# A feed-forward layer's opening inside the mixing's tail, and outputs computed one pair later, on one Trainium2 core

## What is computed

```python
x = x + _L0_attn_ref(_layernorm(x), ...)
x = x + _L0_ffn_ref(_layernorm(x), ...)
x = x + _L1_attn_ref(_layernorm(x), ...)
x = x + _L1_ffn_ref(_layernorm(x), ...)

# first part of layer 0, inside: a recurrence over the tokens, 32 heads, state 32
bc = einsum('bti,oi->bto', value, W_bc)            # then each group of 32 is divided by its norm
z = S * (z - dt * A * s + dt * (Bz * u));  s = s + dt * z + dt * (Bx * u)
y = (Cz . z) + (Cx . s)
return einsum('bti,oi->bto', (y + skip * value) * silu(gate), W_out)

# second part
h = silu((x @ w1) * s1) * ((x @ w2) * s2)          # "up", 128 -> 512
h = gelu((h @ h1) * t1);  h = gelu((h @ h2) * t2)  # 512 -> 512, twice
return (h @ w3) * s3                               # "out", 512 -> 128
```

## Time and profile before

| | us |
|---|---|
| median of 3 runs | 1328.13 |
| lowest and highest of them | 1324.44, 1331.52 |
| the profiled execution | 1331.72 |
| its span, from the first instruction to the last | 1329.6 |
| PE busy in the span | 1279.4 (96%) |
| DVE busy | 910.6 (68%) |
| ACT busy | 651.5 (49%) |
| POOL busy | 588.8 (44%) |

### The profile page before, as it was taken

How to read it: one execution, slowest core, us unless ns; L and a number is a source line. 1 busy time by engine, 2 the same in 40 slices (tenths; PEclk the granted TensorE clock), 3 DMA queues, 4 the chain that set the end, 5 groups by cost and what they waited for, 6 DMA issues and landing times. The chain is left out here.

```text
span 1329.6 us, 23001 instructions
## 1 busy us (share of the span) xinstructions
PE 1279.4 (96%) x7802; PEld 705.5 (53%) x7802; DVE 910.6 (68%) x1771; ACT 651.5 (49%) x1564; POOL 588.8 (44%) x939
## 2 busy tenths in 40 slices
PE   7999998999999999998899998999999999999999
PEld 4443334566566566565445454555655556544545
DVE  6999996999999999997301206888787786630100
ACT  3265533566665665664322315665565666531221
POOL 2633323888888988987100002444444453500000
PEclk7989999999999999998899999999999999999999
DMA  3369897656656665664100002000000000000000
GB/s 99 127 264 394 338 393 273 215 191 224 201 201 212 220 203 196 223 213 167 64 0 0 1 0 90 1 1 1 1 1 1 2 1 1 1 0 0 16 0 16
DMA packets 72834, 151.38 MB, mean 114 GB/s; under 512 B 7312, under 2 KB 24336, under 8 KB 69904
## 3 DMA queue, kind: packets, MB, share of 16 engines
q1 hardware_dynamic: 66096, 133.66, 28.5%
q10 hardware_dynamic: 6624, 16.26, 3.2%
HBM read 98.78 MB, written 51.12 MB: 113 GB/s over the span
## 5 line engine op out<-in xcount | busy, mean ns | idle before, releaser
L1869 POOL TENSOR_SCALAR pr<-pr,rs,sg 128x512 f32<-128x512 f32 (+3 forms) x256 | 152.6, 614 | 204.9 <-DVE rs L1774 186.1
L720 PE MATMUL banks<-w_bc,valueT 128*128 128x512 f32 x392 | 185.1, 596 | 3.4 <-ACT ent L593 2.4
L1046 DVE TENSOR_TENSOR pp<-banks,ring 128x1024 f32<-128x1024 f32 x128 | 156.1, 1220 | 12.8 <-DVEq L1083 5.5
L1675 ACT ACTIVATE pr<-banks,nm 128x512 f32<-128x512 f32 (+3 forms) x256 | 132.8, 524 | 20.4 <-DVE nm L1768 17.7
L1663 ACT COPY prT<-banks 128x512 f32<-128x512 f32 (+3 forms) x128 | 54.3, 424 | 112.5 <-PE banks L1544 112.3
L1768 DVE TENSOR_REDUCE nm<-banks 128x2 f32<-128x1024 f32 (+3 forms) x128 | 105.5, 824 | 4.4
L1384 DVE TENSOR_TENSOR x<-x,banks 128x256 f32<-128x256 f32 x16 | 6.7, 421 | 148.3 <-PE banks L1295 148.3
L935 ACT COPY qk<-banks 128x512 f32<-128x512 f32 x128 | 74.8, 585 | 63.0 <-PE banks L834 63.0
L672 POOL TENSOR_TENSOR C<-abL,A 128x128 f32<-128x128 f32 x128 | 53.3, 424 | 104.9 <-DVE banks L347 91.8
L1544 PE MATMUL banks<-ident,pr 128*128 128x128 f32 x640 | 96.9, 281 | 2.1 <-POOL pr L1869 0.7
L1130 POOL TENSOR_SCALAR_AFFINE_SELECT bp<-bp 128x1024 f32<-128x1024 f32 x64 | 73.8, 1152 | 55.9 <-ACT bp L942 55.9
(11 more groups left out here) (254 smaller groups left out, 2499.6 us busy)
## 6 DMA issues: line engine op xcount, KB each, us to landing
ring<-psi SPq DMA_DIRECT2D x126, 512.0 KB, 4.4
psi<-ring SPq DMA_DIRECT2D x10, 2048.0 KB, 7.5
psi<-X SPq DMA_DIRECT2D x5, 2048.0 KB, 7.5
det<-w_bc ACTq DMA_DIRECT2D x16, 512.0 KB, 4.7
ring<-det SPq DMA_DIRECT2D x64, 128.0 KB, 4.7
bcs<-ent ACTq DMA_DIRECT2D x30, 256.0 KB, 6.9
ring<-bcs SPq DMA_DIRECT2D x30, 256.0 KB, 5.0
w_bc<-in_w_bc SPq DMA_DIRECT2D x4, 1024.0 KB, 10.9
```

The source lines that it names most:

```text
L720: mm = pe.matmul(bank, m["valueT"][:, c, t * P:(t + 1) * P], w, start=(c == 0), stop=(c == 1))
L1046: dve.tensor_tensor(pp[:, q % 2].rearrange("p (a c) n -> p a c n", c=2), sc.unsqueeze(2).broadcast_to([P, 4, 2, HN]), rec[:, n % RL, q % 2 ...
L1675: act.activation(pr[:, n % RP, h, 0:w], S[n % 2][:, h, 0:w], ACT.Exp, bias=nm[:, n % 4, h:h + 1], accum_out=sm[:, m % 3, n % 2, h:h + 1]). ...
L1869: pool.tensor_scalar(row, row, rs[:, n // 2 % 2, n % 2, h:h + 1], sg[:, TPB * b + it, hd:hd + 1], ALU.mult, ALU.mult).then_inc(s["scaled"], 1)
```

## The change

It has three parts.

**The layer's opening moves into the loop of `mix`**, for the first feed-forward layer only (`OPENED`). The turns of block 0 and 1 (`turn_first`), ScalarE's copies of them (`take_first`), the four up-products of block 0 (`up_first`), silus (`silu_first`) and gates (`gate_first`) are placed in the pairs 61 to 64 and after the loop, in banks 4 to 7. Their results lie in the memory of the ring of records (`opening_parts`), which now outlives `mix`; the second layer's attention uses the same memory for a buffer of its own. `ffn` sets its semaphores as if these steps had been done and begins with the turn of block 2. The first three weight transfers count on a semaphore of their own. ScalarE's square root for the last block moves behind the silus of block 1.

**TensorE's pair** becomes: scores of p, outputs of both units of p-1, first turn of p+1, projection, state and end of a half (even pairs, two pairs later than the half's last unit is put out), second turn, projection (even pairs). The state's transpose and the projection out go to free columns of bank YG. The loops run one pair longer. ScalarE takes YG in even pairs ahead of the copies of turns, spreads the state between the two copies of turns, and gets `expand_u` from GpSimd.

**GpSimd's pair** becomes combine, combine, gating, mask: the mask stands last, the gating (`evacuate`) comes from VectorE, and the factors C have three buffers (RC = 3) in place of two.

In the listings below, names in a row are of the memory that is written and read: `qk` is the scores' matmul, `bp,uz` and `qk,hz` the outputs, `ident,ct` and `ident,bp` a turn, `w_bc,valueT` a projection, `ident,hT` the state's transpose, `w_out,yg` the projection out.

TensorE before, in the middle of the loop: an odd pair, from its scores to the next pair's.

The diff, cut to its core:

```diff
@@ -727,13 +728,17 @@
     EARLY = TILES - TPB
     UNITS = TILES * HG
     PAIRS = UNITS // 2
-    RL, RB, RC, RQ = 3, 3, 2, 4
+    RL, RB, RC, RQ = 3, 3, 3, 4
...
@@ -821,12 +827,6 @@
                 pe.wait_ge(s["bt"], q + 1)
                 if q >= 1:
                     pe.wait_ge(s["qk"], q)
-                if q >= 10 and q % 4 == 2:
-                    t, f, j = split(q - 7)
-                    if passes_on(t):
-                        pe.wait_ge(s["hz"], 2 * (links(t, f) + 1))
-                    if f == 1:
-                        pe.wait_ge(s["oc"], t + 1)
...
                     if q > 0:
                         pe.wait_ge(s["ygc"], q // 4)
-                    if carried(t):
-                        pe.wait_ge(s["hz"], 2 * (links(t - 1, f) + 1))
+                    if q >= 8:
+                        ts, fs, js = split(q - 8)
+                        if passes_on(ts):
+                            pe.wait_ge(s["hz"], 2 * (links(ts, fs) + 1))
+                        if fs == 1:
+                            pe.wait_ge(s["oc"], ts + 1)
...
-                pe.transpose(TP[:, 0:P], hT[:, f].rearrange("p a n -> p (a n)"), k.ident[:]).then_inc(s["turned"], 1)
+                pe.transpose(YG[:, STATE:STATE + P], hT[:, f].rearrange("p a n -> p (a n)"), k.ident[:]).then_inc(s["turned"], 1)
...
+
+            def turn_first(b):
+                pe.wait_ge(s["prod"], UNITS - 2)
+                pe.wait_ge(s["row"], TPB * (b + 1))
+                for t in range(TPB):
+                    mm = pe.transpose(k.bank[4 + b][:, t * P:(t + 1) * P], rows[:, b * TPB + t], k.ident[:])
+                mm.then_inc(s["first_turned"], 1)
+
+            def up_first(c):
+                pe.wait_ge(s["first_xnT"], 2)
+                pe.wait_ge(k.ffn_first, FFN_FIRST)
+                pe.wait_ge(s["prod"], UNITS)
+                if c >= 2:
+                    pe.wait_ge(s["first_gated"], c - 1)
+                for n in range(2):
+                    mm = pe.matmul(k.bank[(6, 4)[c % 2] + n][:], first_w["w12"][:, n, c * P:(c + 1) * P], first_xnT[:, 0:T])
+                mm.then_inc(s["first_up"], 1)
...
-            for p in range(2 - LEAD, PAIRS + 2):
+            for p in range(2 - LEAD, PAIRS + 3):
                 if 0 <= p < PAIRS:
                     scores(2 * p)
                     scores(2 * p + 1)
+                if 1 <= p <= PAIRS:
+                    outputs(2 * p - 2)
+                    outputs(2 * p - 1)
+                if p == PAIRS - 1:
+                    up_first(1)
+                    up_first(2)
+                if p == PAIRS:
+                    up_first(3)
                 for u in range(2):
                     if 0 <= p + 1 < PAIRS:
                         turn_both(2 * p + 2 + u)
                     if 2 <= p + LEAD < PAIRS:
                         project(2 * (p + LEAD) + u)
-                if 0 <= p < PAIRS:
-                    outputs(2 * p)
-                if p >= 3 and p % 2 == 1:
-                    t, f, j = split(2 * (p - 2))
-                    pe.wait_ge(s["qk"], min(2 * p + 4, UNITS))
-                    if passes_on(t):
-                        turn_state(t, f)
-                    if f == 1:
-                        project_out(t)
-                if 0 <= p < PAIRS:
-                    outputs(2 * p + 1)
+                    if p == PAIRS - 3 and u == 0:
+                        turn_first(0)
+                        turn_first(1)
+                    if p == PAIRS - 2 and u == 0:
+                        up_first(0)
+                    if p >= 4 and p % 2 == 0 and u == 0:
+                        t, f, j = split(2 * (p - 4))
+                        pe.wait_ge(s["ygc"], min(p, PAIRS) // 2)
+                        if passes_on(t):
+                            turn_state(t, f)
+                        if f == 1:
+                            project_out(t)
...
+            def expand_u(t):
+                act.wait_ge(s["yg"], HG * (t - 1))
+                for f in range(2):
+                    dst = uz[:, t % 2, f].rearrange("p (j e) -> p j e", e=DIAG)[:, :, 0:P].rearrange(
+                        "p j (i e) -> p j i e", i=4)[:, :, :, 0:DH]
+                    act.copy(dst, m["u"][:, t, f * P:(f + 1) * P].rearrange("p (i j d) -> p j i d", i=4, j=4)
+                             ).then_inc(s["uz"], 1)
+
+            def take_first(b):
+                act.wait_ge(s["first_turned"], b + 1)
+                act.copy(first_xnT[:, b * T:(b + 1) * T], k.bank[4 + b][:]).then_inc(s["first_xnT"], 1)
+
+            def silu_first(c):
+                act.wait_ge(s["first_up"], c + 1)
+                if c >= 2:
+                    act.wait_ge(s["first_gated"], c - 1)
+                act.activation(first_g[:, c % 2], k.bank[(6, 4)[c % 2]][:], ACT.Silu,
+                               scale=first_w["s12"][:, 0, c:c + 1]).then_inc(s["first_silu"], 1)
...
-            for p in range(2 - LEAD, PAIRS + 2):
+            for p in range(2 - LEAD, PAIRS + 3):
                 if 0 <= p < PAIRS:
                     copy_scores(p)
                 if 2 <= p + LEAD - 1 < PAIRS:
                     root(p + LEAD - 1)
+                if 2 <= p <= PAIRS and p % 2 == 0:
+                    take(p // 2 - 1)
                 if 0 <= p + 1 < PAIRS:
                     copy_qk(2 * p + 2)
-                    copy_qk(2 * p + 3)
-                if 2 <= p + LEAD < PAIRS:
-                    square(p + LEAD)
-                if p >= 3 and p % 2 == 1:
-                    t, f, j = split(2 * (p - 2))
+                if p >= 4 and p % 2 == 0:
+                    t, f, j = split(2 * (p - 4))
                     if f == 1:
...
-                        act.copy(oc[:], TP[:, P:2 * P]).then_inc(s["oc"], 1)
-                if 0 <= p < PAIRS and p % 2 == 1:
-                    take(p // 2)
+                        act.copy(oc[:], YG[:, STATE + P:STATE + 2 * P]).then_inc(s["oc"], 1)
+                if 0 <= p + 1 < PAIRS:
+                    copy_qk(2 * p + 3)
+                if p == PAIRS - 3:
+                    take_first(0)
+                    take_first(1)
+                if p == PAIRS - 2:
+                    silu_first(0)
+                if p == PAIRS - 1:
+                    silu_first(1)
+                    silu_first(2)
+                if p == PAIRS:
+                    silu_first(3)
+                if 2 <= p + LEAD < PAIRS:
+                    square(p + LEAD)
+                if p >= 4 and p % 4 == 1 and p // 4 + 1 < TILES:
+                    expand_u(p // 4 + 1)
...
+            def gate_first(c):
+                dve.wait_ge(s["first_silu"], c + 1)
+                dve.scalar_tensor_tensor(out=first_ha[:, 0, c], in0=k.bank[(6, 4)[c % 2] + 1][:],
+                                         scalar=first_w["s12"][:, 1, c:c + 1], in1=first_g[:, c % 2], op0=ALU.mult,
+                                         op1=ALU.mult).then_inc(s["first_gated"], 1)
...
-                    evacuate(t, f)
                 if q % 2 == 0 and q // 2 % 16 == 12 and q // 2 >= 28:
                     invert(q // 32 - 1)
-            evacuate(TILES - 1, 0)
-            evacuate(TILES - 1, 1)
+            for c in range(HID // P):
+                gate_first(c)
...
+            def evacuate(t, f):
+                tok = slice(t * P, (t + 1) * P)
+                pool.wait_ge(s["ygc"], 2 * t + f + 1)
+                if t >= 2:
+                    pool.wait_ge(s["out"], t - 1)
+                pool.tensor_tensor(yg[:, t % 2, f], ygc[:, f, 2 * N:], m["gateT"][:, f, tok], ALU.mult).then_inc(s["yg_done"], 1)
...
             for p in range(-1, PAIRS):
                 if p + 1 < PAIRS:
                     combine(2 * p + 3)
+                if p + 2 < PAIRS:
+                    combine(2 * p + 4)
+                if p >= 3 and p % 2 == 1:
+                    t, f, j = split(2 * (p - 2))
+                    evacuate(t, f)
                 if p >= 0:
                     mask(p)
-                if p + 2 < PAIRS:
-                    combine(2 * p + 4)
                 if p >= 7 and p % 4 == 3:
                     residual(p // 4 - 1)
-                if p >= 4 and p % 4 == 1 and p // 4 + 1 < TILES:
-                    expand_u(p // 4 + 1)
                 if p >= 28 and p % 16 >= 12:
                     normalise(TPB * (p // 16 - 1) + p % 16 - 12)
+            evacuate(TILES - 1, 1)
             residual(TILES - 1)
 
...
-def load_ffn(sp, m, ins, loaded):
+def opening_parts(m):
+    flat = m["ring"][:]
+    slot = 2 * 8 * HN
+    return (flat[:, 0:2 * T].rearrange("p (r t) -> p r t", r=2),
+            flat[:, slot:3 * slot].rearrange("p (b c t) -> p b c t", b=2, c=HID // P))
...
+        sp.dma_start(w["w12"][:, j], ins[n]).then_inc(first, 16)
+    sp.dma_start(w["s12"], ins["s12"]).then_inc(first, 16)
...
+            if OPENED:
+                pe.sem_inc(s["turned"], 2)
+                pe.sem_inc(s["up"], KH)
+            else:
+                turn(0)
+                turn(1)
...
```

(9 more changed lines are left out.)

80 lines of the change are left out of this document (45 added, 35 removed).

## The result

The changed kernel takes **1353.35 us** (median of 6 runs, 1343.66 to 1359.38), the kernel before 1329.89 us in the same comparison (median of 6, 1324.44 to 1336.47): ratio 1.0183, 95% interval 1.0151 to 1.0215. It is 1.8% slower; the forecast was 1319.6 us, and the time lies outside the range of 1310 to 1333. The profiled execution of the changed kernel spans 1351.2 us, that of before 1329.6 us.

A forecast was written before the change was run, and what follows sets the result against it. The prediction took TensorE to bound the loop, 25.48 us a tile. From the profiled 1331.72 us, -9.8 + 2.8 - 1.5 gave 1323.2, and 3.6 less for the median 1319.6 us; range 1310 to 1333.

The forecast's parts named there:

- Part 3: Loop, outputs one pair later: TensorE's floor of 25.48 us a tile stays; 0 us, between -3 and +6.
- Part 5: Loop, gating moved from VectorE to GpSimd: VectorE loses 9.8 us but had time spare; 0 us.
- the cost that could undo this: Loop, shared way to memory: GpSimd operations hold VectorE's scaling L1023, making VectorE the bound; +19 us, chance 0.13.
- TensorE bounds the loop: Mid-loop tile: TensorE busy 25.48 of 25.48 us, VectorE second by 1.3 us a tile.
- Part 1: Opening of the first feed-forward layer: two turns and four up-products leave it; -9.8 us.
- Part 2: Mixing's tail: takes in the opening's 7.9 us of TensorE work, 5.1 covered; +2.8 us, ends +0.5 and +7.9.
- the hitch: Mixing's last 30 us: a VectorE operation took 4.80 us, usually 0.25; forecast to stay; rival that it goes, 1313.5 us, 0.17.
- Part 4: Loop, ScalarE's chain of copies: a draw with TensorE, 0 us; tiles with a batch's moments, -1.5 us.
- The rival's point of decision: Loop: mean time of L1023, 1.03 us, from which VectorE's holding would decide the time; chance of slower 0.13.
- The rival's time: Whole kernel if VectorE, held by GpSimd, needs 26.7 us a tile: +19 us, 1339 us; chance 0.13.

The follow-up runs named there:

- mask_waits: Changed kernel with one wait added: GpSimd's mask waits until VectorE has done the L1085 of that round; 1319.41 us, ratio 0.993.
- loop_only: Changed kernel with the layer's opening left where it was before, so only the loop is changed; 1354.50 us, ratio 1.0212.
- no_hitch: opening_only with four normalisations moved from pairs 60 to 63 to pairs 62 and 63, two each; 1316.63 us, ratio 0.9921.
- opening_only: Kernel before with only the layer's two turns and four up-products moved into the mixing's tail; 1321.76 us, ratio 0.9961.
- write_only: Changed kernel with GpSimd's mask replaced by a fill of zeros that reads nothing; 1316.90 us in one run.
- later_plain: Changed kernel with the mask between the two combines and the gating on VectorE, both as before; 1352.77 us, ratio 1.0175.
- two_buffers: Changed kernel with two buffers of factors instead of three; 1336.63 us, ratio 1.0061.

## Why the prediction was wrong, point by point

- **The step that failed** is the loop's term in the sum. Parts 3 and 5 put the later outputs, the mask at the end of GpSimd's round and the moved gating at 0 us each, and the cost that could undo this was argued away. The loop measured +33.6 us. In the changed kernel the mask starts 0.04 to 0.11 us ahead of L1085 and holds it for nearly all its length, VectorE's products are late, and TensorE idles 2.4 us in a carried tile; one wait that keeps the mask behind L1085 gives 34 us back (1353.35 to 1319.41).
- **TensorE bounds the loop** (first section): right for the kernel before, and right again with mask_waits, 25.40 of 25.46 us busy. In the changed kernel it no longer does.
- **Part 1, -9.8:** right, -9.3 (10.89 to 1.59 us).
- **Part 2, +2.8:** the tail grew by 1.7 us, but by luck: the hitch went at the same time. Against loop_only, where it is gone too, the opening's work costs 4.4 us (26.89 to 31.28); in the old loop, with the hitch in both, 0.45 (29.62 to 30.07). All lie within the stated ends, but for the last, just under +0.5. The working took 4.6 of the 10.5 us of TensorE's idle time as the hitch's, where the earlier trace rows give 3.15 in its window; without the hitch the tail of no_hitch is 4.3 us shorter than that of opening_only.
- **Part 3, later outputs, 0:** right as a statement on TensorE's parts: carried tiles of 25.45 us stand in mask_waits and write_only. Wrong as a price: with the mask and the gating where they were (later_plain), 31 us are lost against opening_only. It counted what the mask may wait for, "so the mask can stand last", and not what it meets; put last it costs 23 us.
- **Part 4, ScalarE's chain:** TensorE's wait for the even pair's copy did not come. The -1.5 for the tiles with moments did not come either. These are three sets of two tiles; before they took 51.8 us each, with mask_waits 51.6, 52.3 and 52.1 in order of time.
- **Part 5, the gating, 0:** mis-sized, in the other direction. On GpSimd instead of VectorE the gating gains 21 us with the mask last (1373.92 to 1353.35), 23 with it between the combines (1352.77 to 1330.18), 8 with the wait (1327.64 to 1319.41), and nothing in the loop of before (1316.63 and 1317.77). The third buffer, which was to pay for the mask standing last, costs 17 us there (1336.63 to 1353.35). The sign set down for part 5, TensorE waiting for VectorE's products in every tile, is what the trace shows: 18 times in 280 us, 22.1 us.
- **The cost that could undo this** named the right operation and the right mechanism and gave it 0.13. Its argument against, "L1023 comes after a root, and a block of 0.73 us is what most GpSimd operations can give", failed: it took the two engines as independent, so that a mask would be met by chance. They are coupled by waits, and with 2.06 and 2.26 us between common points they meet in the same phase in most rounds.
- **The rival's point of decision**, a mean of 1.03 us, was set too high. The loss was there at 0.947 us, since it left out the state's operations: L1117, L1121 and L1127 took up to 0.65 + 0.72 + 0.70 instead of 0.21 + 0.29 + 0.29 us, 1.28 us a set, with two sets a tile. It also took TensorE as waiting only when VectorE's sum passes its own; but TensorE waits in the even pair although VectorE has 1.2 us left in the tile (27.24 of 28.41).
- The rival's time, 1339 us, was 14 us short of 1353.35.
- **The hitch**: left where it is by the forecast. In fact it went in the tail, and two of the same kind came in the loop, 4.74 us each, at 445.39 and at 558.56.

## What to carry to other kernels

Where VectorE is within some per cent of the bound and GpSimd runs beside it, list VectorE's small SBUF operations with what GpSimd has running at their start, in the new order; a small operation costs what it meets, and not its own time. Look for the wait that couples the two engines and add up both ways from there: if the two ways end at the same moment, here within 0.04 us, what meets once meets in most rounds, and a single wait that orders the two can be worth more than the whole change. Such a wait is cheap only where the held-back result isn't wanted soon: here +44 us with outputs in the same pair and a combine behind the mask, -34 us with outputs one pair later and the mask last. And vary the parts in a square before calling them dependent: here two parts of 21 to 23 us nearly cancelled, and a third of 31 us stood behind them.

## What the runs showed of the hardware that was not expected

- A VectorE operation can be held over many GpSimd operations and not over one: 4.74 us over seven (445.39), 4.80 us in the kernel before and in opening_only. It is rare. In the changed kernel from pair 0 on, a VectorE operation that had waited over 0.02 us was let in at 118 of 130 ends of a GpSimd operation with another one right behind it; the 12 others all belong to the two holdings of 4.74 us. In the records GpSimd's next operation starts a little before the last one's end: 0.05 us or less at most of the 118, 0.05 to 0.07 at the 12. But in two_buffers operations stayed held at 0.03 to 0.06 us, so this doesn't separate the cases, and what sets it is open.
- A one-input tensor_scalar on 128x32 fp32 is held as the two-input form is: 1.15 us for 0.17.
- The reciprocal right behind it (L1088, one input in SBUF) was never held: 0.353 us in the mean in every kernel.
- A fill of zeros by GpSimd over 128x1024 takes 0.95 us and held none of the ten scalings that began within it; a mask over the same takes 1.15 us and holds them.
